# Second attention: the transposed columns of a unit stored side by side, and the moving operand of the values product read permuted

## What is computed

```python
dots = einsum('bhid,bhjd->bhij', l2norm(q), l2norm(k)) * QK_SCALE   # k, v: 4 memory rows in front
dots = einsum('hg,bgij->bhij', W_pre_th, dots)                      # heads mixed
...                                                                 # causal mask, top 64 of each row kept
attn = softmax(dots, axis=-1)
attn = einsum('hg,bgij->bhij', W_post_th, attn)                     # heads mixed again
out = einsum('bhij,bhjd->bhid', attn, v)
out = out * head_scale_params ... * sigmoid(x @ Wg + bg)
return out @ Wo
```

## Time and profile before

| | |
|---|---|
| runs | 3330.03, 3333.95, 3338.43 us; median 3333.95 |
| profiled execution | 3324.31 us, span of the instructions 3322.4 us |
| second attention, first to last maximum of DVE (L1306) | 1105 to 3052 us of the span |
| one batch in it, batches 1 to 6 | 245.8 us each |
| granted TensorE clock, mean | 0.912 of 2.4 GHz |

### The profile page before, as it was taken

The page is one execution under the profiler, slowest core; times in us unless marked ns, Lnnn a source line. Parts: engine busy times, 40 slices in busy tenths (PEclk is TensorE's granted clock), DMA queues, the critical chain, the costliest instruction groups (busy, mean ns, idle before and its releaser), DMA issues. The chain is left out here.

```text
span 3322.4 us, 60231 instructions
## 1 busy us (share of the span) xinstructions
PE 2737.8 (82%) x19012; PEld 1644.5 (49%) x19012; DVE 2312.3 (70%) x7740; ACT 2211.2 (67%) x5521; POOL 1238.4 (37%) x3658
## 2 busy tenths in 40 slices
PE   3788888888888788888888888888888888876898
PEld 1233333333334455555556556556556556555565
DVE  3545444535422589799799898898888888887465
ACT  0245555455543688788788888888888888885331
POOL 2111101101000355565565565565565565574000
PEclk6689989888899799999999999999999999987899
DMA  2111011101100110110110210110210110111442
GB/s 90 37 33 40 19 22 39 36 8 36 48 4 7 50 38 29 53 38 29 58 35 27 59 37 25 58 37 24 61 38 22 57 38 26 55 46 38 92 97 65
DMA packets 111298, 137.16 MB, mean 41 GB/s; under 512 B 20448, under 2 KB 90592, under 8 KB 110464
## 3 DMA queue, kind: packets, MB, share of 16 engines
q1 hardware_dynamic: 110976, 133.25, 14.7%
HBM read 47.62 MB, written 13.24 MB: 18 GB/s over the span
## 5 line engine op out<-in xcount | busy, mean ns | idle before, releaser
L1242 ACT ACTIVATE junk<-xs,thr 128x420 bf16<-128x420 f32 (+12 forms) x832 | 466.0, 571 | 24.4 <-POOL thr L957 19.8
L1070 PE MATMUL pm<-mixin,pre_b 128*128 128x258 f32 (+15 forms) x1088 | 370.4, 459 | 89.0 <-ACT xs L1235 84.8
L1083 PE MATMUL pt<-wsc,attn 128*128 128x128 f32 x2560 | 360.3, 289 | 97.1 <-ACT at L1261 60.0
L1083 PEld LDWEIGHTS pt<-wsc,attn 128*128 128x128 f32 x2560 | 323.3, 197 | 188.1 <-POOL wsc L938 106.4
L615 DVE TENSOR_REDUCE row_max<-po 128x1 f32<-128x384 f32 (+3 forms) x352 | 209.5, 637 | 285.8 <-PE po L457 284.8
L1261 ACT COPY at<-pt 128x128 f32<-128x128 f32 (+3 forms) x512 | 332.0, 759 | 104.0 <-PE po L1121 87.2
L1036 PE MATMUL pa<-kT,qT 64*128 64x258 f32 (+3 forms) x1280 | 301.8, 466 | 99.8 <-ACT arena L1204 64.7
L1364 DVE MAX8 best<-left 128x8 f32<-128x420 f32 (+12 forms) x832 | 368.5, 483 | 0.0
L1204 ACT ACTIVATE arena<-pa,nrm 128x258 f32<-128x258 f32 (+3 forms) x640 | 273.0, 477 | 98.1 <-PE pa L1036 96.0
L1394 DVE SCALAR_TENSOR_TENSOR attn<-xs,bound,ex 128x420 f32<-128x420 f32 (+14 forms) x480 | 226.9, 501 | 121.8 <-issue 74.8
L1070 PEld LDWEIGHTS pm<-mixin,pre_b 128*128 128x128 f32 x1088 | 179.1, 203 | 220.3 <-issue 201.3
(11 more groups left out here) (235 smaller groups left out, 6117.4 us busy)
## 6 DMA issues: line engine op xcount, KB each, us to landing
spread<-gates_dram SPq DMA_DIRECT2D x32, 512.0 KB, 8.1
mixin<-arena SPq DMA_DIRECT2D x32, 258.0 KB
mixin<-arena SPq DMA_DIRECT2D x32, 242.0 KB
mixin<-arena SPq DMA_DIRECT2D x32, 226.0 KB
mixin<-arena SPq DMA_DIRECT2D x32, 210.0 KB
mixin<-arena SPq DMA_DIRECT2D x32, 194.0 KB
parts_dram<-parts SPq DMA_DIRECT2D x16, 384.0 KB, 4.4
q_stack<-parts_dram SPq DMA_DIRECT2D x96, 64.0 KB
```

The costliest lines, as they stand in the source:

```text
L1070: ins = nc.tensor.matmul(bank[:, 0:jn], pre_b[:, :], mixin[:, m % MIX_SLOTS, j0:j0 + jn], start=True, stop=not last)
L1083: ins = nc.tensor.matmul(bank[:, P * k:P * k + P], attn[:, m % A_SLOTS, P * k:P * k + P], wsc[:, m % A_SLOTS], start=True, stop=True)
L1242: ins = nc.scalar.activation(junk[:, z, 0:width(n)], xs[:, m % X_SLOTS, 0:width(n)], ACT.Sign, scale=-1.0, bias=thr[:, s % LIVE, z:z + 1], ...
```

## The change

ACT writes the 8 rows of a unit next to each other: unit u of the block has the places 8u to 8u+7 of each head, in `at2` and (u of the group of 4) in `tail`. Inside a head the order is now (group, unit, row of the unit), where it was (group, row of the unit, unit), the order of the rows. The product with the values reads its moving operand through a permuted view (group, row, unit), so that its columns, the output in PSUM and all that follows stay as they were. Within a group of 32 the moving operand is then read at the places 0, 8, 16, 24, 1, 9, 17, 25, ...: each element is 32 bytes from the one before, or 92 bytes back. The view of the output (`in_rows`) has the same three dimensions and is contiguous. No instruction, wait or buffer is added or removed.

```diff
+            def by_rows(units):
+                return units.rearrange("p (g u j) -> p g j u", u=GROUP, j=R8)
+
+            def in_rows(out):
+                return out.rearrange("p (g j u) -> p g j u", u=GROUP, j=R8)
...
-                                ins = nc.tensor.matmul(bank[at:at + HD1, col:col + RB], vx[:, k, HD1 * h:HD1 * h + HD1], at2[:, k, h, :],
+                                ins = nc.tensor.matmul(in_rows(bank[at:at + HD1, col:col + RB]), vx[:, k, HD1 * h:HD1 * h + HD1], by_rows(at2[:, k, h, :]),
                                                        start=k == 0, stop=k == t and not odd)
...
-                                ins = nc.tensor.matmul(bank[at:at + HD1, col + RB - GROUP * R8:col + RB], vx[:, t + 1, HD1 * h:HD1 * h + HD1],
-                                                       tail[:, h, :], start=False, stop=True)
+                                ins = nc.tensor.matmul(in_rows(bank[at:at + HD1, col + RB - GROUP * R8:col + RB]), vx[:, t + 1, HD1 * h:HD1 * h + HD1],
+                                                       by_rows(tail[:, h, :]), start=False, stop=True)
...
-                        nc.scalar.copy(at2[:, 0:t + 1, :, every(u)],
+                        nc.scalar.copy(at2[:, 0:t + 1, :, R8 * u:R8 * u + R8],
                                        banks_t[T.bank(m)][:, 0:P * (t + 1)].rearrange("p (k h i) -> p k h i", k=t + 1, h=H1)).then_inc(t_free, 1)
...
-                            ins = nc.scalar.copy(tail[0:MEM, :, every(n % GROUP)],
+                            ins = nc.scalar.copy(tail[0:MEM, :, R8 * (n % GROUP):R8 * (n % GROUP) + R8],
                                                  bank[0:MEM, P * z:P * z + P].rearrange("p (h i) -> p h i", h=H1))
```

## The result

The changed kernel takes 3396.8 us (median of four runs, 3395.2 to 3400.2) against 3336.2 for the kernel before (median of four, 3330.0 to 3339.0). The ratio is 1.0186, with a 95% interval of 1.0168 to 1.0203: slower, by 62 us (the medians differ by 61). The forecast was slower by 30.

The account below looks back on a forecast made before the run. In the attention DVE, ACT and PE are nearly level (87, 84, 84%), with PE and ACT waiting for each other. 3324.3 - 50 + 80 = 3354, plus 9.7 for the runs' median: 3364 us, range 3275 to 3475.

Parts of the forecast that it names:

- the price of a lone element: Values product on PE: each permuted element costs 1.75 ns per column in each stream, 56 ns per record instead of 32.3.
- ACT's factor of two: Copies on ACT: 1.75 ns per element at one element per 16 bytes against 0.84 contiguous, carried over to PE's read.
- ACT's term: Copies to `at2` and `tail`: 164 us of ACT time saved, of which 50 us reach the time, bounds 20 and 80.
- the bound of 131: Copies on ACT: lower bound of the saving, 131 us, from busy time per copy with the tail.
- The share: Attention: at equal load a third of ACT's saved time reaches the time, 54 of 164 us, taken as 50.
- PE's term: Values product: the permuted read adds 127 us of PE time, of which 80 us reach the time, bounds 51 and 114.
- the share of 0.63: Values product: part of PE's added time that reaches the kernel's time, 80 us; bounds 0.4 and 0.9.
- Free reads: Rival, L1116 and L1121: PE reads the permuted operand at 32.3 ns per record as now; 3289 us; chance 28%.
- The dearer step: Rival, values product: a step of 32 bytes costs more than 16, 84 ns per record; 3463 us; chance 10%.
- The shared path: Rival, values product: the two streams take turns on one path, 112 ns per record; 3594 us; chance 15%.
- The point from which the sign turns: Values product: below 48 ns per record, 1.5 ns per column and stream, the changed kernel is faster, above it slower.
- ACT's wait for the product's end: ACT's first copy of the next block waits for L1121, 85.3 us in 31 pieces, longer if PE slows.

Follow-up runs that it names:

- ACT's half: Changed kernel with the values product reading `at2` and `tail` contiguously, so a block's rows come out in another order: 3292.5 us, ratio 0.9888 to the kernel before.
- PE's half: Changed kernel with ACT writing strided as before and the values product still reading permuted, so wrong rows are multiplied: 3454.4 us, ratio 1.0372 to the kernel before.

## Why the prediction was right and wrong

**Right: the signs, and the price of a lone element.** The copies came out at 589, 501, 395 and 288 ns against 600, 494, 383 and 277 forecast. The product came to 60.8 ns per record against 56: ACT's factor of two at a step of 16 bytes holds for PE's read, at 1.9 ns instead of 1.75. The Trainium skill (SBUF — State Buffer, the note on cachelines) says this: two hits on a 16-byte line are needed. The trace agrees on both engines: on PE's read a step of 8 bytes is free (32.7 ns) and 16 and 32 bytes cost about double (60.4 and 60.8), on ACT's write 8 bytes are free (600 ns) and 16 cost 1096.

**Wrong: two terms of the sum, both in the same direction.** The net of +30 was a small difference of two larger terms, and it came out at +62: 13 us from ACT's term, 19 from PE's.

- *ACT's term* was -50 and measured -37. The step that failed is "I take 164, since neighbours overlap in the means": the size of the saving. ACT's busy time fell by 117 us. By its own measure, the rows' busy time, the bound of 131 came out at 152, so it was too low and not too high. What neither way of counting had is that a strided copy overlaps what follows it by 0.22 us and a contiguous one by 0.12. That makes up some 29 of the 35 us between 152 and 117; the rest is in ACT's other instructions. The share was right: 0.32 of 117, with 0.3 of 164 forecast.
- *PE's term* was +80 and measured +99 on top of the fast copies. The record was mis-sized, 60.8 ns against 56 (tail 30 against 28), which makes 154 us by spacing where 127 were forecast. With that the share of 0.63 was right too (0.65). Counted by the product's busy time the increase was 141 us, nearer to the forecast, and then the share of 0.70 is the larger error. The spacing took the full clock for the whole attention, in the forecast as in the 154.

That -37 and +99 make +62 proves nothing, as the 99 is what the change leaves beside the run of ACT's half. Taken alone PE's half costs 124. The forecast gave each half a share without saying on top of what; that its shares fit this order of counting is partly luck.

**The rivals.** Free reads: fell with 60.8 ns. The dearer step: fell with the step of 16 bytes, which costs as much as 32; the Trainium skill's page Vector Engine (DVE) Microarchitecture Reference (section 5.2) gives 2.50 ns for a step of 24 words on DVE, and no run here read with such a step throughout. That section also asks, for DVE, for runs of two adjacent words; on PE's read and on ACT's write a step of 8 bytes was enough. The shared path: fell with the run of one permuted head. The point from which the sign turns was put at 48 ns per record; no kernel ran near it: 48 records at the full clock took 1.55 to 1.57 or 2.85 to 2.93 us, 33 or 59 to 61 ns each.

**Where it passed on.** I had ACT's wait for the product's end as the main way in which PE's time reaches the rest. The wait grew as forecast (85.3 to 135.3 us), but moving the product so that the wait shrank didn't help: ACT then waited for the scores. The forecast named the scores on PE's queue but didn't list ACT's wait for them, 83.5 us, which grew by 57 us in the change, where the wait for L1127 grew by 50. ACT's wait for the product was a sign and not the cause.

## What to carry to other kernels

A permutation between two engines has to be paid where it is free: here PE's write to PSUM, or steps of at most 8 bytes on both sides for fp32, and not a step of 16 bytes or more on ACT's write or PE's read of SBUF. Before moving a stride from one engine to another, look at whether some layout gives both sides two elements per 16 bytes. Where a change takes from one engine and gives to another of nearly the same load, the net is small and each term's error is as large as the net; size terms by the engine's busy time, with what neighbours overlap, and say on top of what each is counted.

## What was not expected of the hardware

PE writes fp32 output columns with a step of 16 bytes to PSUM at the pace of contiguous ones (48 records in 1.55 us both ways). The Trainium skill (PSUM — Partial Sum Buffer, the specifications' row on cachelines) says that any non-contiguous pattern slows matmuls significantly; the trace does not agree for this write. Two products that share the array by halves of its columns read their moving operands independently, and one slow stream holds the other to its pace (59.4 ns per record with one of the two permuted, 60.8 with both). The pace of PE's permuted read hardly depends on the granted clock: records of 512 columns at a step of 32 bytes start 913 to 940 ns apart at the full clock and 940 ns at the lower level (one group of four), where contiguous ones go from about 455 to 855 (one group).
